# Four-layer kernel on one core: the first 18 score pairs of batch 0 and the first shift made inside the last batch's expert sums and norms, and the exponentials starting in the second weight buffer

## The reference, cut to what matters

```python
# layer 2 (first experts)
expert_outputs = einsum('bsd,eod->bseo', x, W) + b
output = sum(selected * topk_scores[..., None], axis=2)
x = _layernorm(x + output)
# layer 3 (attention), per batch and head, t = 1024, hd = 8
xn = layernorm(x) * ln_g + ln_b ;  q, k, v = xn @ w_qkv + b_qkv
scores = einsum('bhqd,bhkd->bhqk', q, k) * hd ** -0.5
attn = softmax(scores + relative_bias, axis=-1)
out = einsum('bhqk,bhkd->bhqd', attn, v) @ w_out + b_out
x = _layernorm(x + out)
```

## Time and profile before

| | us |
|---|---|
| median of 3 runs | 1620.78 |
| lowest and highest | 1610.31, 1621.64 |
| the profiled execution: time, span | 1606.27, 1604.4 |
| TensorE busy, VectorE busy, ScalarE busy | 1361.5, 1105.3, 834.9 |

### The profile page before, as it was taken

How to read it: one execution, slowest core, us unless ns; L and a number is a source line. 1 busy time by engine, 2 the same in 40 slices (tenths; PEclk the granted TensorE clock), 3 DMA queues, 4 the chain that set the end, 5 groups by cost and what they waited for, 6 DMA issues and landing times. The chain is left out here.

```text
span 1604.4 us, 20599 instructions
## 1 busy us (share of the span) xinstructions
PE 1361.5 (85%) x7224; PEld 615.1 (38%) x7224; DVE 1105.3 (69%) x2093; ACT 834.9 (52%) x1634; POOL 313.6 (20%) x440
## 2 busy tenths in 40 slices
PE   5679898888979876899999999999999999982660
PEld 2455573656557554122222333233332333222340
DVE  5738549666864556888888888888888887923115
ACT  5226116323430322377777776777777777771225
POOL 3322312322130200000000110421104111053351
PEclk9779899999989967699999999999999999996795
DMA  3070000200020465110011110111101100000224
GB/s 115 2 177 14 1 1 1 80 31 1 1 97 1 52 100 199 35 21 12 11 21 22 38 22 1 37 32 38 21 13 27 24 2 1 1 7 24 62 83 155
DMA packets 45963, 63.50 MB, mean 40 GB/s; under 512 B 8706, under 2 KB 33869, under 8 KB 44022
## 3 DMA queue, kind: packets, MB, share of 16 engines
q1 hardware_dynamic: 42790, 57.97, 14.8%
q0 software_dynamic: 3072, 4.23, 0.8%
HBM read 33.07 MB, written 31.15 MB: 40 GB/s over the span
## 5 line engine op out<-in xcount | busy, mean ns | idle before, releaser
L579 PE MATMUL ps<-space 128*32 128x512 f32 (+5 forms) x4608 | 856.6, 479 | 51.2 <-DVE space L1824 24.6
L2058 DVE TENSOR_REDUCE smax<-ps 128x1 f32<-128x1024 f32 x512 | 604.7, 1219 | 114.4 <-PE ps L579 108.3
L1331 ACT ACTIVATE space<-ps 128x512 f32<-128x512 f32 x1024 | 555.4, 594 | 229.4 <-PE ps L579 228.8
L579 PEld LDWEIGHTS ps<-space 128*32 128x32 f32 (+5 forms) x4608 | 249.5, 110 | 633.7 <-ACT space L1331 328.6
L1429 POOL TENSOR_SCALAR eps_sum<-mv 128x4 f32<-128x4 f32 x32 | 7.4, 230 | 628.0 <-DVEq L1689 627.5
L1202 ACT ACTIVATE btok<-ps 128x128 f32<-128x128 f32 x32 | 8.9, 278 | 170.2 <-issue 76.4
L579 PE MATMUL ps<-w_exp,space 128*128 128x128 f32 x512 | 89.5, 332 | 0.0
L579 PEld LDWEIGHTS ps<-w_exp,space 128*128 128x128 f32 x512 | 77.2, 233 | 17.9 <-issue 17.9
L1783 DVE SCALAR_TENSOR_TENSOR space<-space,conv_w 128x512 f32<-128x512 f32 x96 | 74.8, 787 | 2.3
L1531 POOL DMA_INDIRECT expert_in<-space,slot x64 | 63.0, 984 | 37.6 <-issue 19.3
L1914 DVE TENSOR_TENSOR space<-xnT,ps 128x512 f32<-128x512 f32 x64 | 42.2, 683 | 36.3 <-PE ps L579 36.3
(11 more groups left out here) (247 smaller groups left out, 1472.0 us busy)
## 6 DMA issues: line engine op xcount, KB each, us to landing
q_rows<-space SPq DMA_DIRECT2D x24, 256.0 KB, 2.5
k_rows<-space SPq DMA_DIRECT2D x24, 256.0 KB, 2.8
space<-k_rows SPq DMA_DIRECT2D x16, 384.0 KB, 5.2
space<-q_rows SPq DMA_DIRECT2D x16, 384.0 KB, 6.9
expert_out<-x_all SPq DMA_DIRECT2D x2, 2048.0 KB, 20.0
space<-expert_out SPq DMA_DIRECT2D x4, 1024.0 KB, 8.8
v_rows<-space SPq DMA_DIRECT2D x4, 668.0 KB, 3.3
space<-v_rows SPq DMA_DIRECT2D x4, 668.0 KB, 6.6
```

Source lines behind the costliest of these rows:

```text
L579: return nc.tensor.matmul(out, lhsT, rhs, start=first, stop=last)
L1331: nc.scalar.activation(prob[:, QUAD * (step % PROB_SETS) + unit % QUAD, :], bank(STB + unit % 2), ACT.Exp)\
L2058: v.tensor_reduce(smax[:, N % 2, i:i + 1], ps[:, b0:b0 + 2, :].rearrange("p k n -> p (k n)"), AX.X, ALU.max).then_inc(S.s_max, 1)
```

## The change

Batch 3's expert sums each get one score pair of batch 0 behind them on TensorE (pair k after sum k), and each `expert_step(3, k)` from k = 2 on gets the maximum of pair k - 2 behind it on VectorE. Pair 14's maximum stands behind `expert_added(3, 1)`. Pair 15's maximum and the cut of the first shift stand in the last step of SLOTS between batch 3's second `expert_norm` and its `tail_norm`, and pair 16's maximum, the copy of the turned shift and pair 17's maximum behind `tail_norm`. On TensorE pairs 16 and 17 and the first shift's transpose (into bank 4) stand ahead of the turning of batch 3's rows. SP stores and loads the first shift ahead of batch 3's `store_rows`. TensorE's wait for the position rows and the mixer's end moves to pair 0. ScalarE no longer waits for batch 3's row stores before its first exponential; it waits for them before the first copy of an output (`evac_pv(0)`). The exponentials take the buffers in the order 1, 2, 3, 0, since buffer 0 lies over rows that are still in use. Counts of matmuls and maxima are unchanged.

```diff
+PAIRS_AHEAD = 18
+MAX_LAG = 2
@@ SP
+                if q == B - 1:
+                    shift_rows_back(0)
                 if q is not None:
                     store_rows(q)
...
             for N in range(B * HALVES):
-                shift_rows_back(N)
+                if N > 0:
+                    shift_rows_back(N)
@@ TensorE
+                if kh == 0 and pair == 0:
+                    pe.wait_ge(S.x1_ready, 2 * B)
+                    pe.wait_ge(S.pos_back, POS_BACK)
...
+            def score_ahead(pair):
+                for kh in range(2):
+                    score_matmul(pair, kh)
...
+                if q == B - 1:
+                    for pair in range(2 * E, PAIRS_AHEAD):
+                        score_ahead(pair)
+                    shift_transpose(0)
                 if q is not None:
                     rows_turned_tail(q)
...
                             expert_sum(p, k)
+                            if p == B - 1:
+                                score_ahead(k)
...
-            for pair in range(16 + LEAD):
-                for kh in range(2):
-                    score_matmul(pair, kh)
-                if pair == 16 + LEAD // 2:
-                    shift_transpose(0)
+            for pair in range(PAIRS_AHEAD, 16 + LEAD):
+                score_ahead(pair)
@@ ScalarE
-                nc.scalar.activation(prob[:, QUAD * (step % PROB_SETS) + unit % QUAD, :], bank(STB + unit % 2), ACT.Exp)\
+                nc.scalar.activation(prob[:, QUAD * ((step + 1) % PROB_SETS) + unit % QUAD, :], bank(STB + unit % 2), ACT.Exp)\
@@ VectorE
+                    if q == B - 1 and n == 4:
+                        pair_max(2 * E - 1)
+                        cut_shift(0)
                     if q is not None and n == 4:
                         for H in range(2):
                             tail_norm(q, H)
+                    if q == B - 1 and n == 4:
+                        pair_max(2 * E)
+                        evac_shift(0)
+                        pair_max(2 * E + 1)
...
                             expert_step(p, k)
+                            if p == B - 1 and k >= MAX_LAG:
+                                pair_max(k - MAX_LAG)
...
+                if p == B - 1:
+                    pair_max(2 * E - 2)
```

More of the change, by code:

```diff
@@ L493, in values_of, with shift_rows_back @@
                 sp.dma_start(v_now[:, b % 2].rearrange("p t n -> p (t n)"), v_rows[b]).then_inc(v_back[b % 2], 16)
+            def shift_rows_back(N):
+                sp.wait_ge(S.shiftT_sb, N + 1)
+                sp.dma_start(shift_rows, shiftT[:]).then_inc(S.shift_stored, 16)
+                sp.wait_ge(S.shift_stored, 16 * N + 16)
+                q, qh = (N % HALVES) // 2, N % 2
+                sp.dma_start(AQ[SCORE_ROWS:SCORE_ROWS + SHIFT_PARTS, QUAD * q:QUAD * q + QUAD, qh * HALF:(qh + 1) * HALF],
+                             shift_rows.rearrange("(s h q) n -> s h (q n)", s=SHIFT_PARTS, h=QUAD))\
+                    .then_inc(S.shift_back, 16)
             for s, (m, p, q) in enumerate(SLOTS):
@@ L806, in expert_sum, with score_matmul, tbank, shift_transpose @@
                 last.then_inc(S.xs_used, 1)
+            def score_matmul(pair, kh):
+                N, i = pair // 16, pair % 16
+                b, n = N // HALVES, N % HALVES
+                head, b0 = QUAD * (n // 2) + i // HT, SB + 2 * (i % 2)
+                if kh == 0 and pair == 0:
+                    pe.wait_ge(S.x1_ready, 2 * B)
+                    pe.wait_ge(S.pos_back, POS_BACK)
+                if kh == 0 and pair >= 2:
+                    pe.wait_ge(S.s_max, pair - 1)
+                if kh == 0 and n % 2 == 0 and i == 0:
+                    pe.wait_ge(rows_back[n // 2], 2 * 16 * (b + 1))
+                q0 = (n % 2) * HALF + (i % HT) * P
+                mm(bank(b0 + kh), AQ[0:SCORE_ROWS, head, q0:q0 + P], BK[0:SCORE_ROWS, head, half(kh)]).then_inc(S.s_psum, 1)
+            def score_ahead(pair):
+                for kh in range(2):
+                    score_matmul(pair, kh)
+            tbank_turns = [0]
+            def tbank():
+                if tbank_turns[0]:
+                    pe.wait_ge(S.tbank_free, tbank_turns[0])
+                tbank_turns[0] += 1
+            def shift_transpose(N):
+                pe.wait_ge(S.shift_cut, N + 1)
+                if N > 0:
+                    tbank()
+                nc.tensor.transpose(bank(run_bank(N) if N > 0 else STB)[0:SHIFT_PARTS * 16, 0:P // 2].bitcast(BF16),
+                                    shift16[:].rearrange("p s n -> p (s n)"), ident16[:])\
+                    .then_inc(S.shiftT_psum, 1)
             pe.wait_ge(S.consts, N_CONSTS)
@@ L1286, in evac_pv @@
                     act.wait_ge(S.pvT_psum, N)
+                else:
+                    act.wait_ge(S.rows_stored, ROW_STORES * B)
                 nc.scalar.activation(pv_sb[:], bank(run_bank(N)), ACT.Copy).then_inc(S.pv_evac, 1)
@@ L1963, in expert_step, with pair_max, cut_shift, evac_shift @@
                     expert_added(b, 0)
+            def pair_max(pair):
+                N, i = pair // 16, pair % 16
+                dve.wait_ge(S.s_psum, 2 * pair + 2)
+                b0 = 2 * (i % 2)
+                v.tensor_reduce(smax[:, N % 2, i:i + 1], ps[:, b0:b0 + 2, :].rearrange("p k n -> p (k n)"),
+                                AX.X, ALU.max).then_inc(S.s_max, 1)
+            def cut_shift(N):
+                dve.wait_ge(S.s_max, 16 * N + 16)
+                v.tensor_scalar(shift16[:, 0, :], smax[:, N % 2, :], -1.0, None, ALU.mult).then_inc(S.shift_hi, 1)
+                dve.wait_ge(S.shift_hi, N + 1)
+                v.scalar_tensor_tensor(shift16[:, 1, :], smax[:, N % 2, :], -1.0, shift16[:, 0, :],
+                                       ALU.mult, ALU.subtract).then_inc(S.shift_cut, 1)
+            def evac_shift(N):
+                dve.wait_ge(S.shiftT_psum, N + 1)
+                if N > 0:
+                    dve.wait_ge(S.shift_stored, 16 * N)
+                v.tensor_copy(shiftT[:], bank(run_bank(N) if N > 0 else STB)[0:SHIFT_PARTS * 16, 0:P // 2].bitcast(BF16)).then_inc(S.shiftT_sb, 1)
+                if N > 0:
+                    dve.wait_ge(S.shiftT_sb, N + 1)
+                    dve.sem_inc(S.tbank_free, 1)
             input_norm(0)
@@ L2170, in after_attention @@
                     dve.sem_inc(S.tbank_free, 1)
-            for pair in range(16 + LEAD + 16 * HALVES * B):
+            for pair in range(PAIRS_AHEAD, 16 + LEAD + 16 * HALVES * B):
                 if pair < 16 * HALVES * B:
@@ L2176, in _ @@
                         cut_shift(pair // 16)
-                if pair == 16 + LEAD // 2:
-                    evac_shift(0)
                 if pair >= 16 + LEAD:
```

34 lines of the change are left out of this document (2 added, 32 removed).

## The result

The changed kernel takes 1626.07 us (median of 8 runs, 1615.15 to 1632.32), the kernel before 1613.58 in its 8 (1609.02 to 1621.64). The ratio is 1.0071, with a 95% interval of 1.0042 to 1.0100: some 11 us slower, where I had forecast 5 us faster. That is the rival on the other side, the half clock that stays. The absolute time lies inside my 1604 to 1628 by luck: I had started from a median of 1620.78, and 8 runs put the kernel before at 1613.58. The change itself, +11 us, is larger than any case that I had reckoned with (-12 to +9).

The account below looks back on a forecast made before the run. VectorE's maxima were taken to bound the attention's opening, TensorE and its clock to decide the expert sums. 17.3 + 2.1 - 24.1 = -4.7, taken as -5 us: 1616 against a median of 1620.78, range 1604 to 1628.

Parts of the forecast that it names:

- the half clock that stays: Rival: stalls and waits for maxima keep most expert sums at clock 0.50; +7 to +9 us, 1628 to 1630, chance 0.14.
- With the wait, I let it rise at 600: Expert sums: after TensorE's 3.8 us wait before pair 0, the clock rises at 600 us, during the third sum.
- the 55 that I had named as the sign of a slower kernel: Sign in the changed profile: expert sums taking over 55 us from the first input mean a slower kernel.
- bounds of -12 and +7: Total change with the sums' clock risen at 595.3 and never fallen (-12 us), or half throughout (+7 us).
- Sums +17.3: Batch 3's expert sums, with a pair behind each, end 17.3 us later, at 632.2 instead of 614.90.
- The half-clock bound: Expert sums at half clock throughout, 3.44 us a step: they end 29.0 us later, total +7 us.
- Norms +2.1: Batch 3's norms: two maxima and the cut on VectorE, less idle time, make its rows 2.1 us later.
- Opening -24.1: Attention's opening: the first weight matmul starts at 640.6 instead of 664.68, 24.1 us earlier.
- Start of the loop 0 with up to +2: Attention loop's start: period left alone, but a later clock rise there costs up to 2 us more.
- The wait before sum 8: TensorE idles 2.5 us for the first half's adding, against 0.78 before, and the clock falls again.
- The rule against this reading: Only long idle gaps lower the clock, so 2.5 us before sum 8 would leave it full; total near -12.
- clock holds: Rival: full clock holds from its first rise in the expert sums on; -12 us, 1609, chance 0.22.

Follow-up runs that it names:

- mm_only: Kernel before plus the change's score matmuls behind batch 3's sums and the wait for quad 0, results unused, no maxima added; sums took 58.89 us.
- mm_f32: mm_only with two f32 matmuls of 128 rows and 128 columns in place of each pair's matmuls; sums took 38.23 us.
- mm_bf16: mm_only with eight bf16 matmuls of 128 rows and 128 columns, on constant tiles, in place of each pair's matmuls; sums took 38.61 us.
- b_again: The kernel before profiled once more, no edit; sums took 27.37 us, the four touched stages 93.4 us.
- first4: Changed kernel with pairs beginning only behind sum 4, two in the norms, first shift made where it was before; sums 41.7 us, four touched stages 98.5 us.
- held4: first4 with the maxima of pairs 2 and 3 moved behind the first half's adding; ratio to the kernel before 0.9965 (0.9924 to 1.0007).
- fill_wait: Changed kernel with three unused f32 matmuls of 512 columns between sum 0 and pair 0; ratio to the kernel before 1.0015 (0.9981 to 1.0049).
- first8: Changed kernel with pairs only behind sums 8 to 15, two in the norms; four touched stages 90.2 us, timed ratio to the kernel before 0.9984.
- first4_again: first4 profiled once more, no edit; sums took 41.4 us, the four touched stages 97.7 us.
- max_only: Kernel before plus the change's maxima alone on VectorE behind batch 3's expert inputs, results unused; sums took 29.67 us.
- fill8: first8 plus five unused f32 matmuls of 512 columns in TensorE's idle time behind the routing logits; ratio to the kernel before 0.9983 (0.9950 to 1.0016).
- first16: Changed kernel with no pairs in the sums, only two in the norms; sums took 27.4 us, the four touched stages 94.0 us.
- quad_first: Changed kernel with quad 0's keys and queries loaded ahead of the position rows; sums took 57.76 us.
- fill_quad: quad_first plus five unused f32 matmuls of 512 columns in TensorE's idle time behind the routing logits; sums took 57.63 us.

## Why the prediction was wrong

**The step that failed** is the clock in the expert sums: "With the wait, I let it rise at 600". It didn't rise until 652.6, in the last sum and behind the last gate rows. The sums took 58.16 us from the first input, past the 55 that I had named as the sign of a slower kernel. I had reckoned both ends (bounds of -12 and +7 for full and half clock, the loss coming out near +10) and took the middle by the rises of the kernel before. (The second of those I misread, too: 610.1 is 11 us behind the restart at 598.97, not 7 to 10.) Those rises were made by a different stream, gate rows and sums alone. Put the score pairs in, and the same sums no longer raise the clock (mm_only), while other fillings of the same length do (mm_f32, mm_bf16). My argument against the half clock, that TensorE has no waits at 3.44 us a step, was true in the trace (3.40 us, busy without a gap) and of no use: a gapless TensorE didn't bring full clock here. So the rival that came true had the wrong cause. It laid the half clock on stalls and on waits for maxima. But there were no waits behind pair 0, mm_only has no maxima, and mm_f32 and mm_bf16 stalled longer before pair 0 and rose. I had the hint in hand, since the paced pairs of the opening stood at 0.50 for 30 us with TensorE busy 1.90 of 2.00, and I put that down to the pace.

**The terms**, forecast and measured in the first pair of profiles:
- Sums +17.3, measured +25.95 (against b_again's 27.37 it would be +31). The half-clock bound gave +29.0. Pair 0's wait was 2.79, not 3.8, a step 3.40 and not 3.44, the last two sums have no gate rows, and the last ran partly at full clock. The other way, the biases took 1.87 us at half clock (627.12 to 628.99), where the bound had 1.3.
- Norms +2.1, measured +3.3: the two maxima and the cut stand where I said, and the rest is the half clock of batch 3's projection (671.62 - 666.58 = 5.0 us for the queries' and keys' matmuls, against 629.97 - 625.89 = 4.1 before).
- Opening -24.1, measured -24.25. SP's two DMAs were issued at 666.76 and 668.13, ahead of the stores at 671.99, and no engine waited for the values, as worked out.
- Start of the loop 0 with up to +2, measured +1.77: half clock until 690.1, 7 us after the first exponential instead of 3.
- The wait before sum 8: forecast 2.5 us and a fall of the clock behind it. At half clock there was none. In first4 it was 0.67.

**The rule against this reading.** In held4 and fill_wait the clock fell behind waits of 0.34 and 0.67 us. The rule of the Trainium skill (TensorE: Matmul & The Clock Gate, Why this matters for your kernels), which names only long idle gaps between bursts of matmuls, doesn't account for these falls any more than for the one before the change.

**The rest.** The rival "clock holds" was partly right about the mix at full clock (first8: 15 us at 1.00 with pairs, but a fall behind sum 8 in first4, held4 and fill_wait) and wrong about the way there. The absolute numbers: the median of before came to 1613.58 over 8 runs, 7 below the 1620.78 that I started from, so my 1616 was 10 short of 1626.07.

**What stays open.** Why the clock falls behind sum 8. With score pairs behind sums 4 to 7 it did so in four of four (first4, first4_again, held4, fill_wait). With none there yet it fell in three of seven: in before, max_only and fill8, not in b_again, first16, first8 and first8_timed. In those seven the clock had been up for 7.4 to 9.4 us when sum 8's biases began where it fell, and for 6.5 to 6.9 us where it held. That fits a timing against the last rise, and no run varied it. The biases' matmuls of 8 rows stand there too, but no run took them away. What pairs change is the time down: 20.5 us in the five falls with pairs behind them, 10.2 and 3.5 us in before and max_only.

## What to carry to other kernels

Before moving TensorE work into another stage, look at which clock that stage has and what raises it: here two bf16 matmuls per sum kept 50 us of a gapless stage at half clock and turned a saving of 24 us into a loss of 10. A rise of the clock read in the old trace belongs to the old stream of matmuls. When such a forecast hangs on the clock, take the end at which the moved work has been seen before (these score matmuls at 0.50 for 30 us), and try the work where the clock has already risen (first8), though fill8 shows that the clock can be lost there too. And profile the kernel before twice, since one profile's lucky or unlucky clock was worth 5 us in a stage here and 12 us ahead of it.

## What the runs showed of the hardware that was not expected

- TensorE busy 48.00 of 48 us (quad_first) at a granted 0.50. With eight short bf16 or two f32 matmuls in place of two long bf16 ones the clock rose within 6 us and held for 25.
- The same mix at full clock kept it for 15 us (first8), 10 us (first4), 15 us (fill_wait). Behind a fall it stayed at 0.50 for 20.5 us (first4, held4, fill8, fill_wait).
- The part ahead of batch 3's sums, on TensorE the same instructions in all kernels but fill8 and fill_quad, took 582.7 to 603.2 us, with a mean granted clock of 0.89 at the short end and 0.85 at the long one.
- The part behind the opening took 923 us on some chips and 958 to 966 on others. In the long ones ScalarE waits 17 to 32 us for a release named "remote"; in the short ones (before, after, first4_again, held4) it never does.
- One DMA issue held SP's queue for 41 to 45 us behind the thirteen position DMAs, in every profile (43.44 in the changed kernel). Reordering them only swapped which load pair 0 waited for.
